# One scan over 1024 columns for the two units of a pair, with its schedule set anew

## The chip, the cores and the metric

The kernel runs on one core of one Trainium2 chip. The metric is the device time of one execution in microseconds (us); given are the median and the span of three runs, and one profiled execution. A measurement of this kernel can tell a difference of about 1%.

## The reference, cut to what matters

A batch of 8 sequences (512 positions of width 256) goes through four layers: linear attention (layer 0), two state-space layers (1 and 2), linear attention again (3). Nearly all the work lies in the state-space layers. There, 512 channels of 16 states each follow a recurrence over the 512 positions:

```
dt = softplus(einsum(dt_r, dt_proj_w) + dt_proj_b)
A = -exp(A_log)
def step(h, inp):
    dA = exp(dt_t[:, :, None] * A)
    h = h * dA + (dt_t * u_t)[:, :, None] * B_t[:, None, :]
    y = einsum('bdn,bn->bd', h, C_t)
```

The step has a decay `dA`, an injection `dt*u*B`, and a weighting with `C` that is summed over the 16 states.

## The kernel before, in words

**Units and pairs.** 2 layers x 8 sequences are 16 scans (`SCANS`). The 512 channels are 4 chunks of 128 partitions, taken as two halves of two chunks. A unit is one chunk and one state number: 128 partitions x 512 positions. A scan has 64 units, the kernel 1024. Two units in a row are the two chunks of a half at one state number; they share the rows `B` and `C` and are a pair (512 pairs).

**What a pair costs.** Every pair is of one of two kinds, set by `KINDS` (line 29), which repeats every 16 pairs: 9 are SPREAD and 7 BESIDE. There are three mixing banks in PSUM (`mix`, 512 columns of 128 partitions each, side by side).

- BESIDE: ScalarE writes each unit's decay into a mixing bank (`decay_in_bank`, line 1260). GpSimd multiplies `dt*u` by the B row into the pair's two state buffers (`inject`, line 940, one instruction of 1024 columns). VectorE scans each unit by itself, decay from the bank and injection from the state buffer (`scan`, line 1552).
- SPREAD: ScalarE copies the B row into a bank (`b_row_in_bank`, line 1268) and writes each unit's decay into an SBUF buffer (`decay_beside`, line 1277, `DECAYS` = 7 buffers). VectorE multiplies `dt*u` by the row in the bank into two banks, the row's own last (`inject`, line 1545, 1024 columns), and scans each unit by itself (line 1555).
- Both: GpSimd weights the pair's states with the C row (`weight`, line 949, 1024 columns), and TensorE sums them into the output banks (`sum_up`, line 1915).

**Which bank.** `bank_plan` (line 424) walks through the pairs in order and gives each its banks by which was freed longest ago; a bank is freed by the scan that reads it. `BANK_FREED` is the unit after which a bank may be filled again, and `PRODUCT_LEAD` tells whether a SPREAD pair's product on VectorE is issued one unit early, that is ahead of the last scan of the pair before.

**Order of the work.** Every engine takes its instructions strictly in the order in which the program issues them. That order is written out by tables. A time step is a quarter of a unit. `STEPS` (line 232) says for each fill, copy, product, weighting and sum how many quarter units ahead of or behind its unit it is issued. All else is a chain of named stages: `att` (attention, 16 times), `prep` (a state-space layer up to the step sizes, 16), `tail` (its second half), `post` (its output product and residual, 16) and `setup` (modulation from the condition vector). A chain starts at a base in units, and each of its stages has a number of quarter units behind that. So the place of a stage is 4 x base + its number; unit 0 is at 0. The chains are laid between the units by `run_batches` (line 608). The tables are the output of a planner that is not part of the kernel.

**The opening** runs attention 0, then `prep` 0, whose step sizes end in GpSimd's product `dtu` (`step_sizes`, line 915); only then can the first unit run. Between them lies the setup: for each layer `c0` to `c3` 32 small products on TensorE (line 1592), each followed by `m0` to `m3`, a chain of small VectorE operations (`modulation`, line 1338), and for the state-space layers `g0` and `g1`, 8 products (line 1600), which `mg` on VectorE turns into `gate_nat`. Only after `gate_nat` does SyncE begin to load B and C rows, and does ScalarE fill the first bank. Idle TensorE is filled with products that nobody reads (`fill`, line 1622; `FILLERS`, `PREP_FILLERS`).

**The closing part** runs `post` 15 (out product line 1866, gather, residual line 1532), attention 14's output product and residual (lines 1659, 1485), and the whole of attention 15.

## Time and profile before

| what | us |
|---|---|
| median of 3 runs | 2083.55 |
| lowest, highest | 2068.17, 2085.44 |
| the profiled execution, its own time | 2081.06 |
| its span in the trace, first to last instruction | 2079.2 |
| mean granted TensorE clock | 0.949 of full speed |

The page gives for each engine the time in which it was busy; a group names the source line, the operation, the count, the mean time of one, and the idle time of the engine right before. A timeline row gives the start, the length, how often the instruction follows itself (x2), and in brackets how long the engine had been idle and what released it. Where instructions overlap in the pipeline, a row of x2 is shorter than twice one. Engines: PE is TensorE, DVE VectorE, ACT ScalarE, POOL GpSimd, SP SyncE.

### The profile page before, as it was taken

To read this page: it belongs to the slowest core of one execution; us is meant where nothing else is said; L and a number is where in the kernel's file an instruction comes from. 1 tells how busy PE (TensorE), PEld (TensorE's weight loads), DVE (VectorE), ACT (ScalarE), POOL (GpSimd) and SP (SyncE) were. 2 spreads that over 40 slices of the span, in tenths; PEclk is the share of its full clock that TensorE was granted. 3 is DMA by queue.
4 is the path that set the end of the run, shared out by engine and by line. 5 is a ranking of instruction groups with operands and counts; after the bars stand their busy time and mean duration, and the time that the engine had idled before them with its cause. 6 is when DMAs were issued, how large, how long until landed. Compare 5 with 4: busy or idle time off the path is not lost. (4 is left out here: it accounts for less than half of the span.)

```text
span 2079.2 us, 29187 instructions
## 1 busy us (share of the span) xinstructions
PE 1841.1 (89%) x9282; PEld 1286.2 (62%) x9282; DVE 1781.6 (86%) x1816; ACT 1735.6 (83%) x3242; POOL 1795.5 (86%) x825
## 2 busy tenths in 40 slices
PE   9877798998999999899989989899999989797788
PEld 7545565657666565667667565666667566556566
DVE  5457989998998998899998988999998998898963
ACT  2389888899989899999989889999989898876642
POOL 0058999999998999999998989999998999999960
PEclk9898899999999999999999999999999999897799
DMA  7034444454444544445444535354444544444420
GB/s 271 1 95 148 158 164 156 135 168 152 147 141 150 169 139 162 145 152 173 151 148 145 173 124 181 130 164 164 152 146 147 179 137 148 146 152 154 157 68 21
DMA packets 163785, 302.30 MB, mean 145 GB/s; under 512 B 18904, under 2 KB 27312, under 8 KB 162096
## 3 DMA queue, kind: packets, MB, share of 16 engines
q1 hardware_dynamic: 153110, 287.45, 42.1%
q10 hardware_dynamic: 10522, 12.99, 2.0%
q8 instruction: 75, 1.23, 0.2%
q14 instruction: 78, 0.64, 0.1%
HBM read 292.98 MB, written 5.29 MB: 143 GB/s over the span
## 5 line engine op out<-in xcount | busy, mean ns | idle before, releaser
L949 POOL TENSOR_TENSOR state<-state,c_rows 128x1024 f32<-128x1024 f32 x512 | 1199.6, 2366 | 43.1 <-DVE state L1555 35.5
L1555 DVE TENSOR_TENSOR_SCAN state<-decay,mix_banks 128x512 f32<-128x512 f32 x576 | 674.2, 1207 | 26.5 <-ACT decay L1277 8.3
L1915 PE MATMUL bank<-const_sb,state 128*128 128x128 f32 x4096 | 552.1, 284 | 94.1 <-POOL state L949 93.6
L1915 PEld LDWEIGHTS bank<-const_sb,state 128*128 128x128 f32 x4096 | 485.5, 146 | 204.1 <-POOL state L949 126.2
L940 POOL TENSOR_TENSOR state<-kept,b_rows 128x1024 f32<-128x1024 f32 x224 | 529.9, 2367 | 41.8 <-PE bank L1915 19.6
L1552 DVE TENSOR_TENSOR_SCAN state<-mix_banks,state 128x512 f32<-128x512 f32 x448 | 525.7, 1203 | 45.3 <-ACT mix_banks L1260 33.3
L1277 ACT ACTIVATE decay<-kept,ssm_pack 128x512 f32<-128x512 f32 x576 | 394.5, 715 | 10.8 <-DVE state L1555 7.1
L1545 DVE TENSOR_TENSOR mix_banks<-kept,mix_banks 128x1024 f32<-128x1024 f32 x288 | 353.5, 1228 | 45.7 <-ACT mix_banks L1268 24.1
L1260 ACT ACTIVATE mix_banks<-kept,ssm_pack 128x512 f32<-128x512 f32 x448 | 305.0, 684 | 85.8 <-DVE state L1555 78.9
L967 ACT ACT_TABLE_LOAD x183 | 234.8, 1283 | 37.2 <-DVE prep_minus L1397 17.7
L1797 PE MATMUL bank<-kept,conv_diag 128*128 128x512 f32 x496 | 225.8, 596 | 4.5 <-ACT kept L1204 4.2
L1659 PE MATMUL bank<-att_pack,xnT 128*128 128x256 f32 x704 | 187.6, 410 | 0.0
L1268 ACT ACTIVATE mix_banks<-b_rows 128x512 f32<-128x512 f32 x288 | 167.6, 588 | 11.0 <-DMA b_rows<-flat_rows 5.2
L1659 PEld LDWEIGHTS bank<-att_pack,xnT 128*128 128x128 f32 x704 | 133.1, 200 | 37.0 <-issue 21.3
L1797 PEld LDWEIGHTS bank<-kept,conv_diag 128*128 128x128 f32 x496 | 89.0, 190 | 94.0 <-issue 86.4
L1776 PE MATMUL bank<-kept,ssm_pack 128*128 128x512 f32 x256 | 120.0, 611 | 10.4 <-ACT kept L1178 4.4
L1786 PE MATMUL bank<-ssm_pack,kept 128*128 128x512 f32 x256 | 117.5, 596 | 4.0 <-ACT kept L1195 2.8
L1866 PE MATMUL bank<-gated_w,kept 128*128 128x256 f32 x512 | 115.8, 380 | 3.9 <-ACT kept L1244 3.7
L915 POOL TENSOR_TENSOR kept<-kept 128x1024 f32<-128x1024 f32 x32 | 75.7, 2367 | 46.5 <-ACT kept L1141 45.2
L1866 PEld LDWEIGHTS bank<-gated_w,kept 128*128 128x128 f32 x512 | 95.3, 191 | 16.9 <-issue 4.0
L899 POOL TENSOR_TENSOR att_shift<-att_minus,att_rstd 128x4 f32<-128x4 f32 x32 | 6.6, 207 | 110.1 <-ACT att_rstd L997 110.1
L1776 PEld LDWEIGHTS bank<-kept,ssm_pack 128*128 128x128 f32 x256 | 47.2, 195 | 61.4 <-issue 55.0
(201 smaller groups left out, 2253.9 us busy)
## 6 DMA issues: line engine op xcount, KB each, us to landing
b_rows<-flat_rows SPq DMA_DIRECT2D x512, 256.0 KB, 3.8
c_rows<-flat_rows SPq DMA_DIRECT2D x512, 256.0 KB, 3.5
conv_diag<-conv_diag SPq DMA_DIRECT2D x8, 1024.0 KB, 7.4
out<-x_res ACTq DMA_DIRECT2D x8, 512.0 KB, 3.2
ssm_pack<-ssm_pack SPq DMA_DIRECT2D x2, 1907.0 KB, 12.2
x_next<-x ACTq DMA_DIRECT2D x6, 512.0 KB, 5.2
x_again<-x_dbl ACTq DMA_DIRECT2D x16, 128.0 KB, 2.4
state<-ada_w SPq DMA_DIRECT2D x1, 1536.0 KB, 13.8
```

The lines of the kernel that those rows point to most:

```text
L940: pool.tensor_tensor(pair_states(g), dtu[:, c:c + HC], by_pair(b_rows[:, row % ROWS]), ALU.mult).then_inc(m_inject[BESIDE], 1)
L949: pool.tensor_tensor(st, st, by_pair(c_rows[:, row % ROWS]), ALU.mult).then_inc(m_prod, 1)
L967: act.preload_act_table_set(name)
L1260: act.activation(mix_banks[BANK_OF[g]], dt[:, c, :], ACT.Exp, scale=neg_a[scan_of(si)[0]][:, c * N + n:c * N + n + 1]).then_inc(m_decay[BE ...
L1277: act.activation(decay[:, nth(g) % DECAYS, :], dt[:, c, :], ACT.Exp, scale=neg_a[scan_of(si)[0]][:, c * N + n:c * N + n + 1]).then_inc(m_d ...
L1545: dve.tensor_tensor(both, dtu[:, c:c + HC, :], by_pair(mix_banks[row]), ALU.mult).then_inc(m_inject[SPREAD], 1)
L1552: ins = dve.tensor_tensor_scan(st, mixed, st, 0.0, ALU.mult, ALU.add)
L1555: ins = dve.tensor_tensor_scan(st, decay[:, nth(g) % DECAYS], mixed, 0.0, ALU.mult, ALU.add)
L1659: ins = pe.matmul(dst, lhs[:, c, t * P:(t + 1) * P], weights[:, c, :], start=False, stop=(t % 2 == 1 and c == DC - 1))
L1797: ins = pe.matmul(dst[:, late:], conv_diag[:, c * TAPS + TAPS - 1 - late, :], u[s][:, c, 0:T - late], start=(late == 0), stop=(late == TAP ...
L1866: ins = pe.matmul(dst[:, (t % 2) * D:(t % 2 + 1) * D], lhs[:, c, t * P:(t + 1) * P], weights[:, c, :], start=(c == 0), stop=(c == CH - 1))
L1915: ins = pe.matmul(y_banks[c2][:, t * P:(t + 1) * P], state[:, g % STATES, t * P:(t + 1) * P], ident, start=False, stop=(g == BANK_SUMS[g / ...
```

## The change

The two scans of a SPREAD pair become one instruction over 1024 columns. It runs over the pair's two state buffers, two decay buffers and two mixing banks, each side by side in memory. So that the second unit starts from zero, the first column of every second decay buffer is set to zero once, in the opening, and ScalarE then writes that buffer from column 1 on. For this the decay buffers become 8, and a SPREAD pair's banks must be neighbours: always bank 1 and one of 0 and 2, and the B row goes into whichever of 0 and 2 was freed first. Both banks of such a pair are freed together, at the end of its scan. BESIDE pairs work as before.

All tables of the schedule are new too: the sequence of kinds (still 9 and 7 of 16), the bases, the stages, the steps, the fillers.

```diff
-BANKS, DECAYS, STATES, ROWS = 3, 7, 14, 4
+BANKS, DECAYS, STATES, ROWS = 3, 8, 14, 4
...
-KINDS = (SPREAD, BESIDE, SPREAD, SPREAD, BESIDE, SPREAD, BESIDE, SPREAD, BESIDE, SPREAD, BESIDE, SPREAD, SPREAD, BESIDE, SPREAD, BESIDE)
-FIRST_BASES = {'att': (-60, -28), 'setup': -50, 'prep': -50}
-TAIL_BASE, POST_BASE, PREP_BASE = -7, -46, 9
-ATT_BASES, LATE_BASES = (10, 100, 159, 222), (41, 207)
+KINDS = (BESIDE, BESIDE, SPREAD, SPREAD, BESIDE, SPREAD, BESIDE, SPREAD, BESIDE, SPREAD, SPREAD, BESIDE, BESIDE, SPREAD, SPREAD, SPREAD)
+FIRST_BASES = {'att': (-58, -31), 'setup': -47, 'prep': -52}
+TAIL_BASE, POST_BASE, PREP_BASE = -20, -51, 9
+ATT_BASES, LATE_BASES = (19, 103, 157, 225), (35, 205)
...
-SETUP_STAGES = dict(zip(SETUP_NAMES, (21, 29, 1, 35, 43, 48, 46, 57, 65, 68, 52, 71, 79, 83), strict=True))
+SETUP_STAGES = dict(zip(SETUP_NAMES, (24, 32, 2, 41, 49, 51, 52, 65, 81, 95, 56, 158, 166, 170), strict=True))
...
-FILLERS = {(0, 'turn0'): 18, (0, 'k0'): 20, (0, 'yT0'): 16, (15, 'turn0'): 26, (15, 'k0'): 0, (15, 'yT0'): 23, (15, 'out0'): 0}
-PREP_FILLERS = 10
+FILLERS = {(0, 'turn0'): 33, (0, 'k0'): 0, (0, 'yT0'): 11, (15, 'turn0'): 12, (15, 'k0'): 18, (15, 'yT0'): 3, (15, 'out0'): 5}
+PREP_FILLERS = 12
...
         if pair_kind(p) == SPREAD:
-            of_row[p], scanned["row", p] = first, freed[first]
-            soon = abs(second - first) == 1
-            first, second = second if soon else third, first
-            lead[p] = int(soon)
+            row = min(0, BANKS - 1, key=freed.get)
+            of_row[p], scanned["row", p] = row, freed[row]
+            lead[p] = int(third != 1)
+            first, second = sorted((row, 1))
         for g, k in ((p * HC, first), (p * HC + 1, second)):
             of_unit[g], scanned[g] = k, freed[k]
-            freed[k] = g
+        freed[first], freed[second] = p * HC, p * HC + int(pair_kind(p) == BESIDE)
...
-                act.activation(decay[:, nth(g) % DECAYS, :], dt[:, c, :], ACT.Exp,
+                first = 0 if c2 == 0 else 1
+                act.activation(decay[:, decay_slot(g), first:], dt[:, c, first:], ACT.Exp,
...
                 yield from w.to("mg")
+                dve.wait_ge(s_mask_out, 16)
+                dve.memset(decay[:, 1::2, 0:1], 0.0).then_inc(s_first_decay, 1)
+                dve.wait_ge(s_first_decay, 1)
                 dve.wait_ge(s_gate_rows, 32)
...
-                past(dve, m_scan, BANK_FREED[g] + 1)
+                past(dve, m_scan, max(BANK_FREED[g], BANK_FREED[g + 1]) + 1)
...
+            def scan_pair(g):
+
+                dve.wait_ge(m_decay[SPREAD], nth(g + 1))
+                dve.wait_ge(m_inject[SPREAD], nth_pair(g // HC))
+                for k in range(g, g + HC):
+                    state_free(dve, k - STATES)
+                at = decay_slot(g)
+                dve.tensor_tensor_scan(in_a_row(pair_states(g)), in_a_row(decay[:, at:at + HC, :]), in_a_row(pair_banks(g)), 0.0,
+                                       ALU.mult, ALU.add).then_inc(m_scan, HC)
...
-                if part == PARTS // 2 and is_unit(g):
+                if part == PARTS // 2 and is_unit(g) and kind_of(g) == BESIDE:
                     scan(g)
+                if part == PARTS // 2 and is_unit(g) and kind_of(g) == SPREAD and g % HC == 0:
+                    scan_pair(g)
```

The names of the setup's 14 stages, in the order of the tuple: c0, m0, neg1, c1, m1, perm, g0, c2, m2, g1, neg2, c3, m3, mg. Three more stages of the tables are spoken of below. Attention 0's output product `out0` goes from number 119 to 100, attention 14's from 654 to 659, and its last stage from 667 to 681. `post` 15's `gather0` goes from 215 to 237, and its `add` (the residual of line 1532) from 223 to 257. Among the steps of `bank`, the bank of a BESIDE pair's second unit was filled 7 or 8 quarter units ahead in 138 of 224 cases; now, where a SPREAD pair comes before (160 cases), it is 4 in 75 of them and 2 or 3 in 41.

## Rows read from the trace of the kernel before

**Rows 1.** The page, part 1: busy time of each engine

```profile
PE 1841.1 (89%) x9282; PEld 1286.2 (62%) x9282; DVE 1781.6 (86%) x1816; ACT 1735.6 (83%) x3242; POOL 1795.5 (86%) x825
```

**Rows 2.** Windows, one stage: PE, PEld, DVE, ACT, POOL busy; clock; DMA; GB/s

```profile
700.00:1000.00 300.00, 276.74 (x1448) 193.19 (x1447) 274.61 (x266) 282.80 (x543) 285.13 (x131) 0.98 0.48 156
```

**Rows 3.** Groups by line, the scan loop's and one 512-column VectorE product

```profile
L949 POOL TENSOR_TENSOR state<-state,c_rows 128x1024 f32<-128x1024 f32 x512 | 1199.6, 2366 | 43.1 <-DVE state L1555 35.5 <-DVE state L1552 7.0
L1555 DVE TENSOR_TENSOR_SCAN state<-decay,mix_banks 128x512 f32<-128x512 f32 x576 | 674.2, 1207 | 26.5 <-ACT decay L1277 8.3 <-PE bank L1915 0.5 <-DVE mix_banks L1545 0.4
...
L940 POOL TENSOR_TENSOR state<-kept,b_rows 128x1024 f32<-128x1024 f32 x224 | 529.9, 2367 | 41.8 <-PE bank L1915 19.6 <-DMA b_rows<-flat_rows 18.5 <-DVE state L1552 1.1
L1552 DVE TENSOR_TENSOR_SCAN state<-mix_banks,state 128x512 f32<-128x512 f32 x448 | 525.7, 1203 | 45.3 <-ACT mix_banks L1260 33.3 <-POOL state L940 10.3
...
L1545 DVE TENSOR_TENSOR mix_banks<-kept,mix_banks 128x1024 f32<-128x1024 f32 x288 | 353.5, 1228 | 45.7 <-ACT mix_banks L1268 24.1 <-POOL kept L915 12.4
L1260 ACT ACTIVATE mix_banks<-kept,ssm_pack 128x512 f32<-128x512 f32 x448 | 305.0, 684 | 85.8 <-DVE state L1555 78.9 <-DVE state L1552 5.6
...
L1268 ACT ACTIVATE mix_banks<-b_rows 128x512 f32<-128x512 f32 x288 | 167.6, 588 | 11.0 <-DMA b_rows<-flat_rows 5.2 <-DVE state L1555 3.5 <-DVE state L1552 2.0
...
L1566 DVE TENSOR_TENSOR kept<-bank,kept 128x512 f32<-128x512 f32 x64 | 41.4, 679 | 1.1 <-PE bank L1915 1.1
```

**Rows 4.** Waits: engine, line, releaser; us in total, times, longest

```profile
ACT mix_banks L1260 <- DVE state L1555: 78.9, 59, 3.3
...
POOL state L949 <- DVE state L1555: 35.5, 37, 2.6
...
DVE state L1552 <- ACT mix_banks L1260: 33.3, 35, 2.4
...
DVE mix_banks L1545 <- ACT mix_banks L1268: 24.1, 23, 3.6
...
POOL state L940 <- PE bank L1915: 19.6, 19, 3.5
POOL state L940 <- DMA b_rows<-flat_rows: 18.5, 15, 4.2
...
ACT decay L1277 <- DVE state L1555: 7.1, 4, 2.7
```

**Rows 5.** Timeline of VectorE: start, length, line, count, idle before

```profile
1010.45 1.23 DVE L1545 TENSOR_TENSOR mix_banks<-kept,mix_banks 128x1024 f32<-128x1024 f32 x1
1011.77 2.33 DVE L1555 TENSOR_TENSOR_SCAN state<-decay,mix_banks 128x512 f32<-128x512 f32 x2
1014.02 2.31 DVE L1552 TENSOR_TENSOR_SCAN state<-mix_banks,state 128x512 f32<-128x512 f32 x2
```

**Rows 6.** Timeline of TensorE in the opening

```profile
40.07 4.42 PE L1592 MATMUL bank<-silu_c,state 128*128 128x8 f32 x32
...
54.26 3.64 PE L1592 MATMUL mix_banks<-silu_c,kept 128*128 128x8 f32 x32
...
59.75 3.58 PE L1600 MATMUL mix_banks<-kept,silu_c 128*8 128x256 f32 x8 [0.92 <-DVEq L1355]
63.26 3.96 PE L1592 MATMUL bank<-silu_c,kept 128*128 128x8 f32 x32
67.15 0.60 PE L1655 MATMUL mix_banks<-bias_rows,right_rows 3*128 3x512 bf16 x1
```

**Rows 7.** Timeline of VectorE in the opening

```profile
53.47 1.38 DVE L1402 TENSOR_SCALAR xn<-v,att_minus,att_rstd 128x256 f32<-128x256 f32 x4 [0.59 <-ACT att_rstd L997]
...
126.81 1.23 DVE L1545 TENSOR_TENSOR mix_banks<-kept,mix_banks 128x1024 f32<-128x1024 f32 x1 [12.08 <-POOL kept L915]
```

**Rows 8.** Timeline of GpSimd in the opening

```profile
124.38 2.35 POOL L915 TENSOR_TENSOR kept<-kept 128x1024 f32<-128x1024 f32 x1 [44.02 <-ACT kept L1141]
```

**Rows 9.** Timeline of VectorE in the closing part

```profile
2027.56 0.69 DVE L1532 TENSOR_TENSOR x_res<-bank,x_res 128x512 f32<-128x512 f32 x1 [3.20 <-PE bank L1866]
...
2034.52 0.69 DVE L1485 TENSOR_TENSOR x_res<-bank,x_res 128x512 f32<-128x512 f32 x1 [2.48 <-PE bank L1659]
```

More of the change, by code:

```diff
@@ L232 @@
 STEPS = {
-    "bank": (17, 7, 8, 8, 10, 6, 8, 3, 10, 9, 2, 2, 12, 7, 12, 8, 4, 4, 12, 10, 12, 8, 8, 6, 3, 5, 12, 7, 9, 6, 7,
[14 rows of a table removed]
-    "row": (11, 1, 9, 3, 3, 3, 6, 12, 5, 7, 6, 12, 7, 9, 11, 8, 12, 7, 7, 8, 12, 6, 5, 7, 5, 12, 7, 8, 3, 10, 7, 8,
[8 rows of a table removed]
-    "beside": (2, 5, 15, 17, 9, 11, 20, 22, 30, 2, 1, 5, 16, 18, 19, 21, 29, 31, 42, 41, 33, 36, 37, 37, 43, 38,
[22 rows of a table removed]
-    "inject": (13, 32, 29, 21, 17, 30, 25, 20, 3, 6, 4, 11, 21, 18, 12, 14, 16, 18, 19, 19, 26, 14, 17, 25, 13, 18,
[8 rows of a table removed]
-    "weight": (9, 4, 10, 9, 19, 15, 9, 11, 5, 10, 6, 15, 10, 6, 12, 8, 8, 6, 8, 7, 6, 7, 6, 7, 10, 15, 10, 10, 14,
[18 rows of a table removed]
@@ new lines @@
+    "row": (8, 0, 7, 6, 6, 12, 7, 3, 9, 11, 9, 8, 5, 6, 12, 8, 5, 11, 8, 5, 4, 6, 9, 4, 8, 3, 8, 8, 8, 5, 6, 6, 10,
[8 rows of a table added]
+    "beside": (14, 16, 17, 19, 11, 10, 11, 7, 18, 22, 25, 26, 44, 10, 13, 13, 4, 8, 27, 31, 35, 38, 50, 54, 51, 53,
[22 rows of a table added]
+    "inject": (7, 10, 27, 27, 31, 20, 19, 5, 2, 5, 13, 17, 18, 20, 5, 9, 13, 9, 4, 24, 21, 12, 16, 10, 10, 9, 9,
[8 rows of a table added]
+    "weight": (10, 8, 4, 8, 6, 8, 6, 15, 20, 18, 16, 11, 10, 7, 4, 7, 4, 7, 6, 7, 7, 12, 8, 8, 15, 15, 15, 11, 11,
[19 rows of a table added]
+    "sum": (22, 20, 24, 20, 16, 12, 9, 7, 14, 12, 14, 11, 12, 11, 21, 19, 32, 51, 47, 44, 42, 50, 47, 50, 52, 49,
[39 rows of a table added]
+}
@@ L769, in state_free, with decay_slot, pair_banks, in_a_row @@
                 eng.wait_ge(m_sum, SUM_COUNT[g])
+        def decay_slot(g):
+            return (nth(g) - 1) % DECAYS
+        def pair_banks(g):
+            return mix[:, BANK_OF[g]:BANK_OF[g] + HC, :]
+        def in_a_row(pair):
+            return pair.rearrange("p k t -> p (k t)")
         def pair_states(g):
@@ L1540, in inject, with row_last @@
                     dve.wait_ge(p_dtu, si * HALVES + half + 1)
-                past(dve, m_scan, BANK_FREED[g] + 1)
+                past(dve, m_scan, max(BANK_FREED[g], BANK_FREED[g + 1]) + 1)
                 dve.wait_ge(m_brow, nth_pair(g // HC))
-                at, row = BANK_OF[g], ROW_BANK[g // HC]
-                both = mix[:, at:row + 1, :] if row > at else mix[:, at:(row - 1 if row else None):-1, :]
-                dve.tensor_tensor(both, dtu[:, c:c + HC, :], by_pair(mix_banks[row]), ALU.mult).then_inc(m_inject[SPREAD], 1)
+                row = ROW_BANK[g // HC]
+                def row_last(pair):
+                    return pair[:, ::-1, :] if row == BANK_OF[g] else pair
+                dve.tensor_tensor(row_last(pair_banks(g)), row_last(dtu[:, c:c + HC, :]), by_pair(mix_banks[row]), ALU.mult).then_inc(m_inject[SPREAD], 1)
             def scan(g):
                 st, mixed = state[:, g % STATES], mix_banks[BANK_OF[g]]
-                dve.wait_ge(m_decay[kind_of(g)], nth(g))
-                dve.wait_ge(m_inject[kind_of(g)], nth_pair(g // HC))
-                if kind_of(g) == BESIDE:
-                    ins = dve.tensor_tensor_scan(st, mixed, st, 0.0, ALU.mult, ALU.add)
-                else:
-                    state_free(dve, g - STATES)
-                    ins = dve.tensor_tensor_scan(st, decay[:, nth(g) % DECAYS], mixed, 0.0, ALU.mult, ALU.add)
-                ins.then_inc(m_scan, 1)
+                dve.wait_ge(m_decay[BESIDE], nth(g))
+                dve.wait_ge(m_inject[BESIDE], nth_pair(g // HC))
+                dve.tensor_tensor_scan(st, mixed, st, 0.0, ALU.mult, ALU.add).then_inc(m_scan, 1)
+            def scan_pair(g):
[6 more added lines that the diff above has]
+                                       ALU.mult, ALU.add).then_inc(m_scan, HC)
             def gate(si, half, c2):
```

42 lines of the change are left out of this document (21 added, 21 removed), and 458 rows, old and new, of tables (ATT_STAGES, POST_STAGES, PREP_STAGES, STEPS).

## The prediction

> **What bounds the kernel now.** I read the page's busy times first: GpSimd and VectorE are each busy for 86% of the span, TensorE for 89%, ScalarE for 83% [rows 1]. No engine carries the kernel alone, so I went on to a stage in the middle: there GpSimd is busy for 285.1 of 300 us, ScalarE for 282.8, TensorE for 276.7, VectorE for 274.6 [rows 2]. GpSimd has least room, 5%, and the others 6 to 9%. The groups say what GpSimd does: 512 weightings and 224 injections of 2.37 us [rows 3]. The change alters neither their number nor their size: 7 of 16 pairs stay BESIDE. So the middle can gain at most what GpSimd idles there, and the waits say for whom: 35.5 us for the scans of SPREAD pairs, 19.6 us for state buffers from TensorE, 18.5 us for B rows [rows 4]. That is the reader's first finding: a cheaper scan shortens only the first of these. The waits also show the partner that may take the saving back. VectorE waits 33.3 us (35 times) for a decay in a bank and 24.1 us (23 times) for a copied B row, while ScalarE waits 78.9 us until a scan frees a bank [rows 4]. Two engines wait for each other over three banks.
>
> What lies outside the middle is a chain in which GpSimd is idle: up to the first step sizes at 124.38 us it waits 44 us in a row [rows 8]. The first product of the scan loop on VectorE comes at 126.81 us, after 12.08 us of idling [rows 7].
>
> **The scan.** 576 scans of 512 columns become 288 of 1024. Nothing in the trace scans 1024 columns, so I bound it. A product of 1024 columns over two banks takes 1228 ns, one of 512 columns takes 679 ns [rows 3]: two of the short ones are 2 x 679 - 1228 = 130 ns longer than the long one. If a scan's fixed part is like that, a pair saves 130 ns, 288 x 0.130 = 37 us of VectorE; that is the upper bound. But scans follow each other closer than they are long: two take 1014.02 - 1011.77 = 2.25 us from start to start [rows 5], 1.125 us each, against a mean length of 1.207 us [rows 3]. So 0.082 us of the fixed part already lies beside the next scan, and the net saving is 0.130 - 0.082 = 0.05 us a pair, 14 us in all. The lower bound is 0: the same columns run with one instruction fewer, which excludes a loss in the scan itself (its waits come below). I take 14 us, as the start-to-start rows are of the very instruction.
>
> The Trainium skill has this fixed part too. VectorE: DVE Perf Modes, section on the TRN2 errata, gives a VectorE instruction that reads PSUM 120 cycles besides its columns, at 0.96 GHz 125 ns, and its section on the DRAIN says that the next instruction starts only when the pipeline is empty. By that the estimate is 288 x 0.125 = 36 us. The length agrees with the 130 ns above, but the trace shows scans that start before the one ahead has ended [rows 5], so on the DRAIN the measurement decides.
>
> **The banks.** A SPREAD pair now holds two neighbouring banks until its one scan ends. Before, the first came free 1.125 us sooner. Walking `bank_plan` through the two sequences of kinds: before, a bank was never needed sooner than two scans after it came free, except by VectorE itself. After, two cases are tighter. Where BESIDE follows SPREAD (5 times in 16 pairs) the second unit's bank comes free with the pair's scan and is wanted after one scan of 1.125 us, in which ScalarE must notice, and fill for 0.684 us [rows 3]. Where SPREAD follows two BESIDE (2 in 16) the row's copy of 0.588 us [rows 3] has the same 1.125 us, as the product now goes ahead of the last scan. That is 7 x 32 = 224 tight places with 0.44 to 0.54 us to spare at most. ScalarE takes its work in order, and behind a late fill on VectorE stand the scan, the next product and all later scans; GpSimd's weighting waits for them. A late place costs 33.3 / 35 = 0.95 us [rows 4]. Today 58 of 736 fills and copies come late, 8%. The lower bound is no new late place, as the steps were set anew with 2 to 4 quarter units for these fills; the upper is one in three, 75 x 0.95 = 71 us. I take 12, between the 0 and the 18 that 8% more of these 224 places would give: 11 us. So the scan loop gains 14 - 11 = 3 us.
>
> **Smaller edits.** The joint scan also waits for the second unit's decay and state buffer 1.125 us sooner than before. Behind it on VectorE stands the next product, behind its end GpSimd's weighting. Scans now wait 8.3 us in all for decays [rows 3] and ScalarE 7.1 us for a free decay buffer [rows 4]; an eighth buffer is added and most decays are issued many quarter units ahead. I cost it at 0, between 0 and another 8 us. The missing column and the memset in `mg` lie under VectorE's 12.08 us of idling [rows 7]; 0.
>
> **The opening.** Here the order changes most. In quarter units, `c2` was at 4 x -50 + 57 = -143 and `c3` at -129, ahead of attention 0's `out0` at 4 x -60 + 119 = -121. Now `out0` is at 4 x -58 + 100 = -132, `c2` at 4 x -47 + 65 = -123, `g1` at -93, `c3` at -30: all behind it. In the trace `c2`, `g1` and `c3` took 3.64 + 3.58 + 3.96 = 11.2 us of TensorE between 54.26 and 67.15, where `out0` begins [rows 6], although its input was normalised by 54.85 [rows 7]. `c1`, 4.42 us in front of the attention's y product [rows 6], also goes behind it. So 15.6 us leave the path. Back come `g0` in front of `out0` and `g1` inside `prep` 0, 3.58 us each by the row of `g1` [rows 6]. Net 15.6 - 7.2 = 8 us. `c2` then runs while `prep` 0 is normalised, `c3` while its rows are sent round by DMA; if `c3` isn't hidden, 4 us are lost again. The bounds are 0 and 15.6 us. Fillers are about as many as before in front of the first products (33 + 12 against 18 + 20 + 10); 0.
>
> `gate_nat` moves behind `c3` too. Behind that wait on SyncE stand all B and C rows, and on ScalarE the first bank fill. Both are wanted only with the step sizes at 124.38 us [rows 8]; I cost the move at 0, or at the 4 us of `c3` if it is late.
>
> **The closing part.** Attention 14's `out0` was at 4 x 873 + 654 = 4146, behind the residual `add` of `post` 15 at 4 x 978 + 223 = 4135. Now it is at 4 x 867 + 659 = 4127, in front of `gather0` at 4 x 973 + 237 = 4129 and `add` at 4149. So the 7 us between the residual at 2027.56 and attention 14's own last one at 2034.52 [rows 9] no longer stand between the residual and attention 15; but their 8 + 8 products now run ahead of the gather, where TensorE has few gaps. I take 2 us of the 7; bounds 0 and 7.
>
> **The sum.** From the profiled execution, 2081.06 us: 2081 - 8 - 3 - 2 = 2068 us. Its own time is 2.5 us under the median of the runs shown, and these spread over 17 us, so I take no correction: 2068 us, 0.7% under the median.
>
> **Rivals.** *The saving arrives whole* (faster). No place comes late, and the fixed part is saved at 14 to 37 us: 2081 - 10 - 14 = 2057 to 2034, middle 2045 us. For it: GpSimd's 35.5 us of waiting for SPREAD scans are spread over 37 waits [rows 4], all of which a shorter scan can cut. Against it: its other waits, and the closeness of the scans [rows 5].
>
> *ScalarE comes late at the tight places* (slower). The time is 2057 + 0.95 k us with k late places: slower than before from k = 25, by over 1% from k = 50; at one in three, k = 75, 2128 us. For it: the 78.9 us in which ScalarE waits for scans today [rows 4], with banks held longer by the change. Against it: steps and kinds were laid out for it.
>
> *The opening does not get shorter* (no change). `c3`, `m3` and `gate_nat` hold up the first rows or fills as long as they used to hold up `out0`: 2081 - 3 - 2 = 2076 us.
>
> **How the numbers follow.** Forecast 0.46, whole saving 0.30, late banks 0.14, opening no shorter 0.10. A measurement of this kernel tells about 1%: under 2062.7 or over 2104.4 us. Faster is the whole saving and 0.10 of the forecast, whose own range is 2055 to 2080: 0.40. Slower are the late banks: 0.14. The same: 0.46. The range reaches to the middle of the whole saving and beyond, and to late banks at k = 48: 2035 to 2103 us.
>
> **What would show it.** The group of joint scans: 288 of about 2.28 us, following each other at 2.2. GpSimd's first step sizes at about 116 us instead of 124.38. VectorE's waits for bank fills and row copies at about 69 us instead of 57.4, GpSimd's busy time unchanged. I am wrong if the step sizes come no sooner, if the joint scan is far from 2.28 us, or if those waits fall or double.

## The result and the profile after

The changed kernel takes 2123.33 us (median of 4 runs, 2111.74 to 2125.75), the kernel before 2079.45 us (4 runs beside it). The ratio is 1.0201, with a 95% interval of 1.0166 to 1.0237: 44 us slower, above the predicted range. The ratios of the experiments below are taken likewise, each to runs of the kernel before beside it. The profiled execution took 2125.75 us, with a span of 2123.8 us.

The page, part 1, and the groups by line of the changed kernel (compare [rows 1, 3]; GpSimd's weighting is now L960, its injection L951, the product L1563, ScalarE's bank fill L1271 and row copy L1279, the scan of BESIDE L1569, the joint scan L1578):

```profile
PE 1847.2 (87%) x9244; PEld 1281.6 (60%) x9244; DVE 1771.0 (83%) x1529; ACT 1727.4 (81%) x3227; POOL 1795.0 (85%) x825
```

```profile
L960 POOL TENSOR_TENSOR state<-state,c_rows 128x1024 f32<-128x1024 f32 x512 | 1197.4, 2364 | 70.7 <-DVE state L1569 37.7 <-DVE state L1578 30.2 <-PE bank L1940 2.5
L1578 DVE TENSOR_TENSOR_SCAN state<-decay,mix_banks 128x1024 f32<-128x1024 f32 x288 | 656.9, 2281 | 48.2 <-DVE mix_banks L1563 19.6 <-ACT decay L1289 12.4 <-PE bank L1940 9.1
...
L1569 DVE TENSOR_TENSOR_SCAN state<-mix_banks,state 128x512 f32<-128x512 f32 x448 | 529.0, 1207 | 65.9 <-ACT mix_banks L1271 42.2 <-POOL state L951 21.6
L951 POOL TENSOR_TENSOR state<-kept,b_rows 128x1024 f32<-128x1024 f32 x224 | 527.3, 2363 | 32.8 <-PE bank L1940 25.9 <-DMA b_rows<-flat_rows 4.9 <-issue 1.1
```

Every engine is busy for a little less time or, TensorE, 6 us more; the 44 us are idle time on all of them. The joint scan is 2281 ns long, as forecast, and VectorE's idle time in front of it has grown from 26.5 us [rows 3] to 48.2 us. The waits:

```profile
POOL kept L926 <- ACT kept L1152: 67.8, 13, 48.4
DVE state L1569 <- ACT mix_banks L1271: 42.2, 43, 3.0
...
DVE mix_banks L1563 <- ACT mix_banks L1279: 33.3, 30, 9.4
...
DVE state L1578 <- DVE mix_banks L1563: 19.6, 105, 0.2
```

VectorE waits for fills and copies for 42.2 + 33.3 = 75.5 us, 73 times, against 57.4 us, 58 times [rows 4]. Two waits are new in this view: a pause of 0.19 us between a product and its joint scan (with short scans it is 0.09 us, too short for the view to list), and 67.8 - 48.4 = 19.4 us (12 times) in which GpSimd stands behind softplus with its step sizes.

Where along the kernel the time is lost is read from two stretches, before and after: from the first weighting to the end of the 33rd, and from the 65th to the 385th. First the windows of the kernel before, then of the changed one (columns as in [rows 2]):

```profile
133.80:259.00 125.20, 90.85 (x431) 62.98 (x429) 104.74 (x94) 110.79 (x188) 112.01 (x51) 0.84 0.44 143
371.80:1555.40 1183.60, 1092.54 (x5600) 757.53 (x5600) 1083.82 (x1039) 1103.16 (x2108) 1123.60 (x513) 0.98 0.47 153
```

```profile
127.80:267.50 139.70, 88.71 (x400) 59.52 (x400) 104.51 (x73) 112.53 (x183) 114.17 (x52) 0.79 0.41 130
382.70:1594.70 1212.00, 1106.81 (x5576) 760.55 (x5577) 1072.37 (x852) 1095.42 (x2094) 1118.49 (x510) 0.97 0.47 149
```

The first weighting ends 6 us sooner (127.8 against 133.8). The first scan then loses 14.5 us, the ten scans of the second stretch lose 28.4 us, and from the last weighting to the end it is 75.6 us instead of 71.0.

TensorE's mean granted clock is lower too, 0.79 against 0.84 of full speed in the first stretch (a mix of its two levels, 1.2 and 2.4 GHz) and 0.97 against 0.98 in the second (nearly all at 2.4 GHz), where TensorE is busy 14.3 us longer for 24 products fewer. No run tells whether that adds to the loss or only follows from TensorE's waiting. It is not all of the loss: in the run **after_decay_wait_last** (below) the clock of the second stretch is 0.98, and the stretch is still 1202.0 - 1183.6 = 18.4 us longer than before.

```profile
383.20:1585.20 1202.00, 1097.75 (x5587) 756.71 (x5588) 1071.97 (x853) 1096.64 (x2097) 1118.69 (x511) 0.98 0.46 150
```

### The profile page after: what moved, and what is told of

The parts are those of the page before. It is cut to its first block and busy times, and to the rows that moved or that the text cites. A ratio compares the mean times of both kernels' runs of the same rounds, so it can differ in the third digit from the quotient of the medians.

```text
span 2123.8 us, 28802 instructions
## 1 busy us (share of the span) xinstructions
PE 1847.2 (87%) x9244; PEld 1281.6 (60%) x9244; DVE 1771.0 (83%) x1529; ACT 1727.4 (81%) x3227; POOL 1795.0 (85%) x825
## 5 line engine op out<-in xcount | busy, mean ns | idle before, releaser
L960 POOL TENSOR_TENSOR state<-state,c_rows 128x1024 f32<-128x1024 f32 x512 | 1197.4, 2364 | 70.7 <-DVE state L1569 37.7
L1578 DVE TENSOR_TENSOR_SCAN state<-decay,mix_banks 128x1024 f32<-128x1024 f32 x288 | 656.9, 2281 | 48.2 <-DVE mix_banks L1563 19.6
L1940 PE MATMUL bank<-const_sb,state 128*128 128x128 f32 x4096 | 558.9, 285 | 100.0 <-POOL state L960 99.7
L1940 PEld LDWEIGHTS bank<-const_sb,state 128*128 128x128 f32 x4096 | 491.6, 147 | 216.6 <-POOL state L960 129.4
L1569 DVE TENSOR_TENSOR_SCAN state<-mix_banks,state 128x512 f32<-128x512 f32 x448 | 529.0, 1207 | 65.9 <-ACT mix_banks L1271 42.2
L951 POOL TENSOR_TENSOR state<-kept,b_rows 128x1024 f32<-128x1024 f32 x224 | 527.3, 2363 | 32.8 <-PE bank L1940 25.9
L1289 ACT ACTIVATE decay<-kept,ssm_pack 128x512 f32<-128x512 f32 x576 | 386.8, 712 | 10.5 <-issue 8.2
L1563 DVE TENSOR_TENSOR mix_banks<-kept,mix_banks 128x1024 f32<-128x1024 f32 x288 | 353.4, 1227 | 42.2 <-ACT mix_banks L1279 33.3
L1271 ACT ACTIVATE mix_banks<-kept,ssm_pack 128x512 f32<-128x512 f32 x448 | 299.3, 682 | 100.6 <-DVE state L1578 85.8
L978 ACT ACT_TABLE_LOAD x168 | 215.5, 1283 | 22.6 <-DVE att_minus L1412 14.6
L1279 ACT ACTIVATE mix_banks<-b_rows 128x512 f32<-128x512 f32 x288 | 169.3, 591 | 35.0 <-DVE state L1569 20.7
L926 POOL TENSOR_TENSOR kept<-kept 128x1024 f32<-128x1024 f32 x32 | 75.5, 2359 | 77.2 <-ACT kept L1152 67.8
```

What stands on the lines that cost most here:

```text
L951: pool.tensor_tensor(pair_states(g), dtu[:, c:c + HC], by_pair(b_rows[:, row % ROWS]), ALU.mult).then_inc(m_inject[BESIDE], 1)
L960: pool.tensor_tensor(st, st, by_pair(c_rows[:, row % ROWS]), ALU.mult).then_inc(m_prod, 1)
L978: act.preload_act_table_set(name)
L1271: act.activation(mix_banks[BANK_OF[g]], dt[:, c, :], ACT.Exp, scale=neg_a[scan_of(si)[0]][:, c * N + n:c * N + n + 1]).then_inc(m_decay[BE ...
L1289: act.activation(decay[:, decay_slot(g), first:], dt[:, c, first:], ACT.Exp, scale=neg_a[scan_of(si)[0]][:, c * N + n:c * N + n + 1]).then ...
L1563: dve.tensor_tensor(row_last(pair_banks(g)), row_last(dtu[:, c:c + HC, :]), by_pair(mix_banks[row]), ALU.mult).then_inc(m_inject[SPREAD], 1)
```

## Experiments: code against tables

Theory 1 was that the joint scan holds two banks and ScalarE fills them late; theory 2 that the new tables are the worse part. The change can be cut in two that way: code (joint scan, bank plan, eighth decay buffer) and tables (kinds, bases, stages, steps, fillers).

**joint_on_old_tables**: the new code with the old tables (`KINDS` as below, and in the same way all bases, stages, `STEPS` and fillers).

```
-KINDS = (BESIDE, BESIDE, SPREAD, SPREAD, BESIDE, SPREAD, BESIDE, SPREAD, BESIDE, SPREAD, SPREAD, BESIDE, BESIDE, SPREAD, SPREAD, SPREAD)
+KINDS = (SPREAD, BESIDE, SPREAD, SPREAD, BESIDE, SPREAD, BESIDE, SPREAD, BESIDE, SPREAD, BESIDE, SPREAD, SPREAD, BESIDE, SPREAD, BESIDE)
...
```

> The joint scan, its bank plan and the eighth decay buffer, with every table of the kernel before (kinds, bases, stages, steps, fillers). Theory 1 (the joint scan holds two banks until its one end, ScalarE fills late, and that is most of the 44 us): 2100 to 2130 us, waits of VectorE for bank fills and row copies 75 us or more. Theory 2 (the new tables are the worse part, the joint scan by itself gives VectorE some 10 us and costs few waits): 2065 to 2085 us, those waits at 57 to 65 us.

2265.84 us, ratio 1.0899 (1.0878 to 1.0921): more than either theory allowed, 187 us.

**split_on_new_tables**: the new tables, two scans of 512 columns, and in `bank_plan` each bank released by its own unit.

```
-    dve.wait_ge(m_decay[SPREAD], nth(g + 1))
-    dve.wait_ge(m_inject[SPREAD], nth_pair(g // HC))
     for k in range(g, g + HC):
+        dve.wait_ge(m_decay[SPREAD], nth(k))
+        dve.wait_ge(m_inject[SPREAD], nth_pair(g // HC))
         state_free(dve, k - STATES)
-    at = decay_slot(g)
-    dve.tensor_tensor_scan(in_a_row(pair_states(g)), in_a_row(decay[:, at:at + HC, :]), in_a_row(pair_banks(g)), 0.0,
-                           ALU.mult, ALU.add).then_inc(m_scan, HC)
+        dve.tensor_tensor_scan(state[:, k % STATES], decay[:, decay_slot(k)], mix_banks[BANK_OF[k]], 0.0,
+                               ALU.mult, ALU.add).then_inc(m_scan, 1)
```

> Everything of the changed kernel but the joint scan: a SPREAD pair has two scans of 512 columns one behind the other at the place of the joint one, each waits for its own decay, and its bank is released at its own end. Theory 1: the banks come free sooner again, 2075 to 2090 us, waits of VectorE for bank fills and row copies back at about 57 us. Theory 2: the tables stay, and VectorE's 14 us are lost again: 2120 to 2140 us.

2113.43 us, ratio 1.0164 (1.0144 to 1.0183). Neither theory gave that: with its joint scan taken out, the changed kernel keeps 34 of its 44 us, and it gets no slower, though the scans cost VectorE 13.3 us more again. So the larger part lies outside the joint scan, and the joint scan by itself gains nothing and costs some 10 us at most: the intervals of the two kernels overlap a little. This kernel still has the new bank plan and the eighth decay buffer. The new tables with the old plan weren't run, so the 34 us belong to tables and plan together; "the new tables" below means both.

**before_late_release**: the old kernel, the price of holding alone.

```
+def held(f):
+    return f | 1 if f >= 0 and kind_of(f) == SPREAD else f
...
-    past(act, m_scan, BANK_FREED[g] + 1)
+    past(act, m_scan, held(BANK_FREED[g]) + 1)
...
-    past(act, m_scan, BANK_FREED["row", g // HC] + 1)
+    past(act, m_scan, held(BANK_FREED["row", g // HC]) + 1)
```

> The kernel before with one thing altered: where ScalarE waits for the first unit of a SPREAD pair to free its bank, it waits for the second unit's scan, 1.125 us later, as with a joint scan. Theory 1: that is the price by itself, 2105 to 2125 us. Theory 2: few fills notice, 2080 to 2088 us.

2143.92 us, ratio 1.0323 (1.0303 to 1.0342): 65 us, more than either theory allowed. Its waits:

```profile
ACT mix_banks L1263 <- DVE state L1558: 170.0, 146, 4.4
...
DVE mix_banks L1548 <- ACT mix_banks L1271: 52.7, 41, 4.3
DVE state L1555 <- ACT mix_banks L1263: 49.3, 43, 2.8
```

ScalarE waits for SPREAD scans 170.0 us instead of 78.9, VectorE for ScalarE 102.0 instead of 57.4 [rows 4]. Holding is dear where the steps are not made for it.

**new_plan_split_old_tables**: the old tables with the new bank plan, two scans released singly (the edits of the first two kernels together).

> The tables of the kernel before and two scans of 512 columns a SPREAD pair, released one by one, but the changed kernel's bank plan (the pair always in banks 0 and 1 or 1 and 2, the row in the outer one) and its eighth decay buffer. With every table old, the joint scan cost 187 us, and the late release alone 65. If the plan is harmless and the scan's holding and early waits are the rest: 2079 to 2095 us. If the plan itself (no free choice of bank) is the larger part: 2130 us or more.

2226.12 us, ratio 1.0689 (1.0668 to 1.0710): with the old tables the plan (and the eighth buffer) costs 146 of the 187 us. A joint scan needs two neighbouring banks, so the row may lie in bank 0 or 2 only; walking the new `bank_plan` through the old kinds, the row of 2 in 16 pairs gets a bank that the scan just ahead has freed, where the old plan always had two scans between. Its waits:

```profile
DVE mix_banks L1563 <- ACT mix_banks L1279: 85.6, 79, 4.7
DVE state L1569 <- ACT mix_banks L1271: 79.0, 65, 2.9
...
ACT mix_banks L1271 <- DVE state L1569: 115.6, 62, 2.9
ACT mix_banks L1279 <- DVE state L1569: 55.0, 54, 2.9
```

ScalarE now waits for scans of BESIDE, 170.6 us in all, against 7.6 us before [rows 3]. Under the new kinds no row has less than one scan between. With the new tables the same code takes 2113 us; how much of that difference is due to the kinds and how much to the steps is not shown.

**split_late_release_new**: `held` of above on the new tables with two scans.

> The new tables with two scans a SPREAD pair (2113 us), and ScalarE's waits on a bank of such a pair put to the end of the second scan. If holding is still the price of the joint scan on the new tables, it costs more than the 9 us between that kernel and the changed one, since it has the longer two scans too: 2120 to 2135 us. If the new tables have taken the holding in (fills are due late enough), 2110 to 2117 us.

2115.65 us, ratio 1.0163 (1.0145 to 1.0180), the same as without (1.0164). Holding costs 65 us on the old tables and nothing that can be measured on the new: their steps have taken it in. With that the holding of theory 1 falls for the changed kernel; fills that come late for another reason do not.

**before_new_opening**: the old kernel with the new stages of attention 0, setup and preparation 0, their bases, and the fillers there.

```
-FIRST_BASES = {'att': (-60, -28), 'setup': -50, 'prep': -50}
+FIRST_BASES = {'att': (-58, -31), 'setup': -47, 'prep': -52}
```

> The kernel before with the opening's order of the changed kernel (stages of attention 0, of the setup and of the first preparation, their bases, the fillers there). Both theories: the first step sizes on GpSimd at about 115 us instead of 124.4, and the whole 6 to 10 us shorter, 2070 to 2074 us. The rival is that the gain is lost again within the first scan, as the changed kernel lost 18 us there: 2079 us or more.

2076.96 us, ratio 0.9993 (0.9981 to 1.0004). In its profile the first weighting ends 7.2 us sooner, the 17th already 1.1 us later than before: the gain is lost in the first scan. The time lies between the two forecasts, and the profile speaks for the rival. This kernel loses 8 us in its first scan in that way, the changed one 14.5 us.

**before_new_attention**: the old kernel with all stages, bases and fillers of the attentions from the new tables.

```
-ATT_BASES, LATE_BASES = (10, 100, 159, 222), (41, 207)
+ATT_BASES, LATE_BASES = (19, 103, 157, 225), (35, 205)
...
```

> The kernel before with all stages, bases and fillers of the attentions from the changed kernel, nothing else. If the new places of the attentions in the scan loop are what the new tables lose with two scans (34 us): 2095 to 2113 us. If the loss is in kinds, steps and the preparations: 2072 to 2087 us.

2403.94 us, ratio 1.1553. Outside every expectation, and no measure of the attentions' new places: the tables were set together, and this part of the one among parts of the other is worse than both.

## Experiments: the pauses round the joint scan

On VectorE the two-scan kernel and the changed one run the same sequence at the same place. First two scans, then the joint one (timeline of VectorE):

```profile
433.14 1.22 DVE L1565 TENSOR_TENSOR mix_banks<-kept,mix_banks 128x1024 f32<-128x1024 f32 x1
434.27 1.22 DVE L1571 TENSOR_TENSOR_SCAN state<-mix_banks,state 128x512 f32<-128x512 f32 x1
435.40 2.31 DVE L1579 TENSOR_TENSOR_SCAN state<-decay,mix_banks 128x512 f32<-128x512 f32 x2
437.74 1.23 DVE L1565 TENSOR_TENSOR mix_banks<-kept,mix_banks 128x1024 f32<-128x1024 f32 x1
438.88 0.68 DVE L1502 TENSOR_TENSOR x_next<-bank,x_next 128x512 f32<-128x512 f32 x1
439.65 2.33 DVE L1579 TENSOR_TENSOR_SCAN state<-decay,mix_banks 128x512 f32<-128x512 f32 x2
```

```profile
431.83 1.22 DVE L1563 TENSOR_TENSOR mix_banks<-kept,mix_banks 128x1024 f32<-128x1024 f32 x1
432.96 1.22 DVE L1569 TENSOR_TENSOR_SCAN state<-mix_banks,state 128x512 f32<-128x512 f32 x1
434.09 2.26 DVE L1578 TENSOR_TENSOR_SCAN state<-decay,mix_banks 128x1024 f32<-128x1024 f32 x1
436.39 1.23 DVE L1563 TENSOR_TENSOR mix_banks<-kept,mix_banks 128x1024 f32<-128x1024 f32 x1
437.52 0.68 DVE L1500 TENSOR_TENSOR x_next<-bank,x_next 128x512 f32<-128x512 f32 x1
438.39 2.29 DVE L1578 TENSOR_TENSOR_SCAN state<-decay,mix_banks 128x1024 f32<-128x1024 f32 x1 [0.18 <-DVE x_next L1500]
```

From the first start to the last end it is 441.98 - 433.14 = 8.84 us with four scans and 440.68 - 431.83 = 8.85 us with two. The joint scans are 0.05 and 0.04 us shorter than their pairs; the second begins 438.39 - 438.20 = 0.19 us behind the addition ahead of it, its pair 439.65 - 439.56 = 0.09 us. The group of the short scans in the two-scan kernel, beside L1578 above:

```profile
L1579 DVE TENSOR_TENSOR_SCAN state<-decay,mix_banks 128x512 f32<-128x512 f32 x576 | 670.2, 1204 | 22.2 <-PE bank L1941 3.9 <-ACT decay L1291 1.5
```

The joint scan saves 670.2 - 656.9 = 13.3 us of busy time and adds 48.2 - 22.2 = 26.0 us of idling. What that idling is can't be read from the releasers of the group: a pause of 0.19 us is put down to whichever wait was fulfilled last, so 16 of the 24 idle times under decays and 22 of the 25 under TensorE (state buffers) are such pauses too, and 30 more have no releaser. Taken one by one by their length, the trace has 173 pauses behind a product, 32.3 us in all, against 182 pauses and 16.3 us with two short scans: 16.0 us more. The longer waits are 9.4 us for decays (8 times) against 1.5, and 4.8 us for state buffers (twice) against 3.9: 8.0 and 0.8 us more, the earlier waits of the second unit. So the pauses alone outweigh the 13.3 us that are saved.

**after_product_wait_last** and **before_product_wait_last**: the order of the waits in front of the scan, here of the changed kernel (before, the one `state_free` moves up likewise).

```
+    for k in range(g, g + HC):
+        state_free(dve, k - STATES)
     dve.wait_ge(m_decay[SPREAD], nth(g + 1))
     dve.wait_ge(m_inject[SPREAD], nth_pair(g // HC))
-    for k in range(g, g + HC):
-        state_free(dve, k - STATES)
```

> The changed kernel with one order altered: the joint scan waits first for its two state buffers and its decays, and last for its product, where it used to wait for decays, product and then the two state buffers. In the changed kernel a joint scan right behind its product begins 0.187 us after the product's end (188 times), with two short scans it is 0.089. If the two waits that stand behind the product's make the difference: 0.09 us or less, 18 us less idling of VectorE, and 2108 to 2118 us. If the pause belongs to the long scan itself: still 0.187, 2119 to 2125 us.

2113.14 us, ratio 1.0178 (1.0155 to 1.0201). Between a product's end and its joint scan there are now 0.132 us (median of the 183 scans that follow their product directly), not 0.187: half of the fall that was expected. The idle time ahead of the joint scan falls from 48.2 to 39.9 us. The pauses are now too short for the view, and the longer waits stand by themselves, 10.7 us for decays and 4.9 us for state buffers:

```profile
L1578 DVE TENSOR_TENSOR_SCAN state<-decay,mix_banks 128x1024 f32<-128x1024 f32 x288 | 657.0, 2281 | 39.9 <-ACT decay L1289 10.7 <-PE bank L1940 4.9 <-DVE x_next L1500 0.4
```

> The kernel before with the same order: a SPREAD unit's scan waits for its state buffer first, then for its decay, last for its product. The pause behind the product is 0.090 us there, 244 times. If the one wait behind the product's makes half of it: 0.04 us, 11 us of VectorE, 2070 to 2078 us. If the pause belongs to the dependence itself: 2076 to 2084 us.

2081.55 us, ratio 1.0019 (1.0005 to 1.0033). A miss: the pause there became longer, 0.132 us instead of 0.090 (median of 242).

**after_decay_wait_last**: state buffers, product, decays.

```
-    dve.wait_ge(m_decay[SPREAD], nth(g + 1))
-    dve.wait_ge(m_inject[SPREAD], nth_pair(g // HC))
     for k in range(g, g + HC):
         state_free(dve, k - STATES)
+    dve.wait_ge(m_inject[SPREAD], nth_pair(g // HC))
+    dve.wait_ge(m_decay[SPREAD], nth(g + 1))
```

> The changed kernel with the joint scan's waits in the order state buffers, product, decays, so that one wait that is long fulfilled stands between the product's and the scan. The pause behind the product was 0.187 us with two such waits behind it, 0.132 with none, 0.090 with one in the kernel before. If the number of waits behind the product's sets it: 0.09 us, 18 us less idling of VectorE than in the changed kernel, 2104 to 2114 us. If the long scan alone makes it longer: 0.13 us or more, 2112 to 2124 us.

2118.75 us, ratio 1.0197 (1.0172 to 1.0222), with a pause of 0.230 us: a miss too.

```profile
L1578 DVE TENSOR_TENSOR_SCAN state<-decay,mix_banks 128x1024 f32<-128x1024 f32 x288 | 656.6, 2280 | 56.2 <-DVE mix_banks L1563 30.3 <-ACT decay L1289 15.0 <-PE bank L1940 9.9
```

So the order of the waits sets the pause (0.132, 0.187 or 0.230 us), but neither the number of waits behind the product's nor the length of the scan tells which. The times of the three versions of the changed kernel don't follow it: VectorE's idle time in front of the joint scan is 39.9, 48.2 and 56.2 us, the intervals of the ratios overlap. The pauses are the larger part of why the joint scan gains nothing on VectorE; they are not the 34 us, which stand without a joint scan.

## Experiments: what the new tables lose

**after_step_sizes_later**, then **after_step_sizes_skips_later**: GpSimd's step sizes moved away from softplus. `LATER` is 1 to 8 by scan; the second kernel moves `skip1` with `mul`, both by 12, and `skip0` and `last` with the first half's.

```
+TAIL_STAGES = {k: {**t, "mul": t["mul"] + 16 * (k > 0)} for k, t in TAIL_STAGES.items()}
...
+PREP_STAGES = {k: {**t, "mul": t["mul"] + LATER.get(k, 0)} for k, t in PREP_STAGES.items()}
```

> The changed kernel with GpSimd's step sizes (the product of dt and u) issued 1 to 8 quarter units later in the first half of each scan from the second on, and 16 later in the second half, behind weightings that are ready. In the changed kernel GpSimd stands 19 us in the middle waiting for softplus there, against 1 us before. If that wait is on the path: 2103 to 2112 us. If GpSimd then waits for the scans instead: 2118 to 2126 us.

2252.60 us, ratio 1.0822. The edit put ScalarE's skip products, which come behind the step sizes, into a wait:

```profile
ACT kept L1163 <- POOL kept L929: 137.8, 22, 11.1
```

> As the kernel with the step sizes later, but ScalarE's skip products, which read the same buffer after the step sizes, are moved by as much (1 to 8 quarter units in first halves, 12 in second halves). In that kernel ScalarE stood 138 us (22 times) behind the step sizes, which hid what the move gives. If the 19 us that GpSimd stands behind softplus are on the path: 2103 to 2114 us. If the next wait takes their place: 2118 to 2126 us.

2128.96 us, ratio 1.0252 (1.0231 to 1.0273). The wait for softplus went, and others took its place:

```profile
POOL kept L929 <- ACT kept L1155: 54.6, 5, 48.5
POOL state L963 <- DVE state L1572: 42.3, 32, 3.9
POOL state L954 <- PE bank L1943: 32.6, 21, 4.6
POOL state L963 <- DVE state L1581: 30.5, 19, 7.3
...
POOL state L954 <- DMA b_rows<-flat_rows: 18.6, 12, 3.1
```

Softplus has 13 us less than in the changed kernel; the rows have 14 us more, TensorE 7, the scans 5. The rival was right in kind, and the time is 3 us above its range.

**after_both_moves**: this and the product's wait last.

> The changed kernel with both, the product's wait last and step sizes and skips later. If both count and add up: 2090 to 2108 us. If either is taken back by the other's wait: 2108 to 2122 us. It stays behind the kernel before unless the loss of the new kinds and steps is smaller than the two short scans show (2113 us).

2126.43 us, ratio 1.0235 (1.0210 to 1.0260): above both ranges, nothing adds up.

**before_short_fills, split_short_fills, after_short_fills**: ScalarE relieved. These leave out half the columns of bank fills and row copies from the 17th pair on.

```
-    act.activation(mix_banks[BANK_OF[g]], dt[:, c, :], ACT.Exp, ...)
+    w_ = T if g < 32 else T // 2
+    act.activation(mix_banks[BANK_OF[g]][:, 0:w_], dt[:, c, 0:w_], ACT.Exp, ...)
...
```

> The kernel before, but ScalarE's bank fills and row copies are 256 columns wide instead of 512 from the 17th pair on (the rest of each bank keeps what stood in it), so ScalarE has some 150 us less to do; waits and order are the same. It is the measure for the two kernels beside it. If ScalarE's lateness binds the kernel before too: 2040 to 2060 us; if not: 2065 to 2079 us.

> The new tables with two short scans a pair (2113 us), fills and copies of 256 columns as beside. If the new tables lose their 34 us because ScalarE comes late: within 12 us of the kernel before with short fills. If the loss lies in the order of the kinds for the other engines: still 22 us or more above it.

> The changed kernel (2123 us), fills and copies of 256 columns as beside. ScalarE's lateness as the loss: within 20 us of the kernel before with short fills, the rest being the pauses round the joint scan. Otherwise: 32 us or more above it.

2057.22 us (ratio 0.9903, 0.9887 to 0.9920), 2088.97 us (1.0055, 1.0040 to 1.0070) and 2097.61 us (1.0099, 1.0080 to 1.0119). In that order the kernels gain 20, 24 and 26 us, and the distances to the first stay nearly what they were: 32 and 40 us instead of 34 and 44. By the expectations that speaks against ScalarE's lateness. But the edit takes only a part of the lateness away: VectorE still waits for fills and copies 38.4 us in the first (23.8 + 14.6), 53.6 us in the second (31.0 + 22.6) and 49.2 us in the third (25.6 + 23.6), where it was 57.4, 84.6 (53.7 + 30.9) and 75.5. So late fills aren't all of what the new tables lose, but up to 15 of the 32 us can still be theirs.

**before_short_gpsimd, split_short_gpsimd**: GpSimd relieved. These leave out half the columns of GpSimd's weightings and injections from the second scan on.

```
...
-    pool.tensor_tensor(st, st, by_pair(c_rows[...]), ALU.mult)
+    w_ = T if g < 64 else T // 2
+    pool.tensor_tensor(st[:, :, 0:w_], st[:, :, 0:w_], by_pair(c_rows[...])[:, :, 0:w_], ALU.mult)
```

> The kernel before, but GpSimd's weightings and injections take 2 x 256 columns instead of 2 x 512 from the second scan on (the other columns of a state buffer stay as they are), so that an operation takes about half its 2.37 us and GpSimd has some 800 us less to do. GpSimd had least room; with it out of the way the other engines set the time: 1950 to 2040 us. It is the measure for the kernel beside it.

> The new tables with two short scans a pair (2113 us), GpSimd's products half as wide as beside. If the new tables lose their 34 us by GpSimd's order: within 17 us of the kernel before with short GpSimd products (15 of the 34 us arise in the opening and the first scan, which stays at full width). If they lose it by the order of the other engines as well: 25 us or more above it.

2089.41 us (ratio 1.0049, 1.0034 to 1.0064) and 2103.38 us (1.0115, 1.0098 to 1.0132). The page, part 1, and GpSimd's first group of the kernel before with short products:

```profile
PE 1842.9 (88%) x9282; PEld 1290.4 (62%) x9282; DVE 1781.6 (85%) x1816; ACT 1735.8 (83%) x3242; POOL 1061.2 (51%) x825
```

```profile
L951 POOL TENSOR_TENSOR state<-state,c_rows 128x512 f32<-128x512 f32 (+1 forms) x512 | 684.9, 1342 | 495.4 <-DVE state L1557 351.4 <-DVE state L1554 135.1 <-PE bank L1917 8.2
```

GpSimd works 734 us less and the kernel before is not faster; it measures 0.5% slower, which is under the 1% that a measurement tells, and why is open. So the forecast of 1950 to 2040 us was a miss. The distance between old and new tables falls from 34 to 14 us, just inside the bound. But only half of that fall is a gain: the kernel with the new tables became 10 us faster, the one it is measured by 10 us slower. So GpSimd's load can't be made out as the cause of a definite share. In the 14 us that are left VectorE waits 54.0 + 29.6 = 83.6 us for fills and copies against 38.9 + 26.3 = 65.2, so late fills stay a candidate there. What in the new tables makes the 34 us is open: the tables could not be taken apart (above), and what was freed at one place was waited for at the next.

## Why the prediction was wrong, point by point

- *The scan's length*: right. 2281 ns; two short ones are 2 x 1204 - 2281 = 127 ns longer, 37 us in all, and 13.3 us of busy time remain where 14 were forecast. The fixed part that the Trainium skill gives in VectorE: DVE Perf Modes, section on the TRN2 errata (120 cycles, 36 us by the estimate), agrees with the 127 ns. The Trainium skill's section on the DRAIN in VectorE: DVE Perf Modes says that the next instruction starts only when the pipeline is empty, by which all of it would be saved; the 13.3 us do not agree with that. The same section adds that an instruction that is not held starts earlier, and here short scans in a row do, 0.08 us before the end of the one ahead [rows 3, 5].
- *"The lower bound is 0 ... which excludes a loss in the scan itself"*: right for the length, but no term of the sum has the pause between the product and the scan. It grew from 0.089 to 0.187 us and takes back 16.0 us, more than the 13.3 us saved. The smaller edits' "0, between 0 and another 8 us" for decays and state buffers measured 8.0 + 0.8 us of idling, at the upper bound.
- *The banks*: the tight places are real, 65 us where the steps ignore them; on the new tables holding has no price that can be measured, where 11 us were forecast. VectorE's waits are 75.5 us, near the 69 forecast, but not for that reason: they are 84.6 us in the kernel with two scans as well (55 + 26 waits), which holds no bank longer. Late fills came with the new tables, not with the holding.
- *The scan loop, "14 - 11 = 3 us" of gain*: this step failed. It priced the scan and the holding, and had no term for the new order of the loop. The new kinds and steps were taken as an answer to the tight places ("the steps were set anew") at no cost of their own. Together with the bank plan that they were made for they cost 34 us with two scans, before the joint scan has done anything. By what mechanism is open; late fills can be a part of it.
- *"The middle can gain at most what GpSimd idles there"*: true as a limit, since GpSimd's work stays the same, but it does not say what sets the length. With 734 us less work on GpSimd nothing was gained; with 1735.6 - 1613.6 = 122 us less on ScalarE (the short fills) the kernel before gained 20 us.
- *The opening, -8 us*: right in place, and near in size: GpSimd's first step sizes come 9.6 us sooner. The size is in part luck. `out0` begins at 56.12 instead of 67.15, 11.0 us sooner, where the terms in front of it gave 15.6 - 3.6 = 12. Its products then take 4.62 us instead of 7.50, at a granted clock of 0.98 (nearly all at 2.4 GHz) instead of 0.58 (mostly at 1.2 GHz, right behind `c2`, `g1` and `c3`): 2.9 us that no term has. 4.4 us are lost again before the step sizes, where 3.6 were forecast. At the end of the kernel the gain is worth nothing (ratio 0.9993). The forecast looked for what the opening saves, not for who is late next: in the first scan ScalarE copies a row at 139.39, behind the next attention's work, and VectorE and GpSimd wait for it.

TensorE at `out0`, before and after (windows, columns as in [rows 2]), then the changed kernel's timelines in the first scan (GpSimd, VectorE, ScalarE):

```profile
67.15:74.65 7.50, 7.50 (x19) 4.69 (x18) 3.22 (x12) 0.00 (x0) 0.00 (x0) 0.58 0.00 0
56.12:60.74 4.62, 4.62 (x22) 3.41 (x21) 0.69 (x1) 0.00 (x0) 0.00 (x0) 0.98 0.00 0
```

```profile
114.83 2.34 POOL L926 TENSOR_TENSOR kept<-kept 128x1024 f32<-128x1024 f32 x1 [48.38 <-ACT kept L1152]
...
143.87 2.36 POOL L960 TENSOR_TENSOR state<-state,c_rows 128x1024 f32<-128x1024 f32 x1 [7.29 <-DVE state L1578]
```

```profile
140.07 1.23 DVE L1563 TENSOR_TENSOR mix_banks<-kept,mix_banks 128x1024 f32<-128x1024 f32 x1 [9.37 <-ACT mix_banks L1279]
```

```profile
137.42 2.06 ACT L1033 ACTIVATE xn<-v,att_shift,att_rstd 128x256 f32<-128x256 f32 x4
139.39 0.58 ACT L1279 ACTIVATE mix_banks<-b_rows 128x512 f32<-128x512 f32 x1
```

- *The closing part, -2 us*: wrong, +4.6. From the normalisation that opens the last attention to its last residual it was 2075.07 - 2039.29 = 35.8 us, and is 2119.62 - 2079.86 = 39.8 us. VectorE waits longer for TensorE at two places, 7.24 instead of 4.69 us and 6.04 instead of 4.63, those of `k0` and `out0`, where the changed fillers of attention 15 (18 and 5 instead of none) stand. In front of `k0` TensorE now runs 36 filler products, 4.18 us, where before it waited 1.23 us for ScalarE. The prediction had weighed the opening's fillers only; these were read from the profiles, not tried alone.

The last attention in the changed kernel, then the same places before (VectorE, and TensorE in front of `k0`):

```profile
2079.86 1.38 DVE L1417 TENSOR_SCALAR xn<-x_res,att_minus,att_rstd 128x256 f32<-128x256 f32 x4 [1.89 <-ACT att_rstd L1008]
2082.22 4.18 PE L1647 MATMUL bank<-const_sb 128*128 128x128 f32 x36
2088.48 0.69 DVE L1454 TENSOR_REDUCE kneg<-mix_banks 128x1 f32<-128x512 f32 x1 [7.24 <-PE mix_banks L1674]
...
2117.38 0.69 DVE L1500 TENSOR_TENSOR x_res<-mix_banks,x_res 128x512 f32<-128x512 f32 x1 [6.04 <-PE mix_banks L1684]
```

```profile
2039.29 1.38 DVE L1402 TENSOR_SCALAR xn<-x_res,att_minus,att_rstd 128x256 f32<-128x256 f32 x4 [1.90 <-ACT att_rstd L997]
2043.05 1.95 PE L1644 MATMUL mix_banks<-xnT,att_pack 128*128 128x512 f32 x4 [1.23 <-ACT xnT L1064]
2045.36 0.69 DVE L1439 TENSOR_REDUCE kneg<-mix_banks 128x1 f32<-128x512 f32 x1 [4.69 <-PE mix_banks L1649]
...
2072.83 0.69 DVE L1485 TENSOR_TENSOR x_res<-mix_banks,x_res 128x512 f32<-128x512 f32 x1 [4.63 <-PE mix_banks L1659]
```

- *The rival of late banks* gave 2128 us, close to the result, by a mechanism that the runs don't bear out for this kernel: it needs 75 more late places by holding, and there are 73 - 58 = 15 more, and 81 - 58 = 23 in the kernel with two scans, which holds no bank longer.
- *"What would show it"*: the signs came out near the forecast: 2281 ns, step sizes at 114.83 us, waits for fills and copies of 75.5 us that neither fell nor doubled, GpSimd busy for 1795.0 us as before. They watched the terms of the sum, and not the term that was missing.

No version tried that does the whole work beats the kernel before; the nearest is its own loop with the new opening, at 0.9993.

## What to carry to other kernels

When an edit comes with a new order of the work, price the order as a term of its own, and measure both crossings: the new code on the old order and the old code on the new. Here the second crossing kept the new bank plan, so it prices order and plan together. An instruction saved is worth what stands between it and its neighbours: look at the pauses round it, not only at its length. An engine that is busy for 95% of a stage need not be the one that sets its length; take half of its work away before a sum is built on it, and look whether the wait that you meant to remove is gone.

## What was not expected of the hardware

The pause between a VectorE operation and one that waits for it is set by the order in which waits stand in front of the second: 0.132, 0.187 and 0.230 us for three orders of the same four waits, 0.090 and 0.132 us for two orders of three. And 734 us less work on GpSimd, with all else alike, did not make the kernel before faster (ratio 1.0049).
